# Sixteen state products of a Mamba layer: four of them moved from VectorE to GpSimd, in a four-part network kernel

## The reference, cut to what matters

```python
xz = x @ in_proj_w.T; xi, z = split(xz)                 # 2 x 256 channels
xc = silu(causal_conv(xi, 4 taps) + conv_b)
xp = xc @ x_proj_w.T                                     # dt_raw, B (16), C (16)
dt = softplus(dt_raw @ dt_proj_w.T + dt_proj_b)
dA = exp(dt * A[n]);  dBx = dt * xc * B[n]               # for each of 16 states n
h_n[t] = dA_n[t] * h_n[t-1] + dBx_n[t]                   # scan over 512 tokens
y = sum over n of h_n * C[n]  + xc * D
out = (y * silu(z)) @ out_proj_w.T
```

## Time and profile before

| | us |
|---|---|
| median of 3 runs | 2473.28 (2472.91 to 2476.75) |
| profiled execution, its own time | 2472.19 |
| its span in the trace | 2470.5 |
| Mamba stage, first scan to last gate product | 550.0 to 1730.9 |
| one pipeline iteration (start of a gate product y2 to the next), 14 of them from 627.63 to 1669.96 | 71.55 to 76.5, mean 74.5 |

### The profile page before, as it was taken

How to read it: one execution, slowest core, us unless ns; L and a number is a source line. 1 busy time by engine, 2 the same in 40 slices (tenths; PEclk the granted TensorE clock), 3 DMA queues, 4 the chain that set the end, 5 groups by cost and what they waited for, 6 DMA issues and landing times. The chain is left out here.

```text
span 2470.5 us, 24903 instructions
## 1 busy us (share of the span) xinstructions
PE 1779.2 (72%) x6321; PEld 937.4 (38%) x6321; DVE 1824.4 (74%) x3163; ACT 947.6 (38%) x1562; POOL 920.8 (37%) x666
## 2 busy tenths in 40 slices
PE   4776103437877677777777777776699999999998
PEld 3454002313333223333323333232455555555555
DVE  4888792128888888788888888889466767666676
ACT  1322000124444555444545445553233433334343
POOL 1101205736576566566575665664000000000000
PEclk7999555569899999898999999999899999999999
DMA  6333102232202122112222011210000000000000
GB/s 171 100 110 97 31 1 35 38 94 77 69 22 82 73 81 81 44 46 77 77 81 81 21 69 77 73 73 5 13 13 14 9 13 13 8 17 8 13 13 9
DMA packets 94551, 125.52 MB, mean 51 GB/s; under 512 B 6576, under 2 KB 86096, under 8 KB 90064
## 3 DMA queue, kind: packets, MB, share of 16 engines
q1 hardware_dynamic: 79888, 115.88, 13.4%
q0 software_dynamic: 14592, 8.92, 2.8%
HBM read 98.81 MB, written 25.90 MB: 50 GB/s over the span
## 5 line engine op out<-in xcount | busy, mean ns | idle before, releaser
L574 POOL TENSOR_TENSOR dbx<-u,ball 128x1024 f32<-128x1024 f32 x256 | 603.7, 2379 | 165.0 <-DVE hst L1293 164.8
L1293 DVE TENSOR_TENSOR_SCAN hst<-bank,dbx 128x512 f32<-128x512 f32 x512 | 598.5, 1210 | 59.5 <-DVE prod L1309 33.5
L744 ACT ACTIVATE bank<-dt,aneg 128x511 f32<-128x511 f32 x512 | 352.3, 690 | 596.4 <-DVE hst L1293 595.0
L966 PE MATMUL bank<-prod,ident 128*128 128x512 f32 x1024 | 531.2, 645 | 16.8 <-DVE prod L1309 16.8
L1309 DVE TENSOR_TENSOR prod<-hst,bank 128x1024 f32<-128x1024 f32 x256 | 311.1, 1215 | 7.9 <-PE bank L966 2.9
L774 ACT ACTIVATE ha<-bank,w_b 128x512 f32<-128x512 f32 (+1 forms) x208 | 142.8, 687 | 409.0 <-PE bank L1034 409.0
L1333 DVE SCALAR_TENSOR_TENSOR hg<-bank,w_b,ha 128x512 f32<-128x512 f32 (+1 forms) x208 | 155.8, 749 | 181.0 <-PE bank L1036 128.2
L966 PEld LDWEIGHTS bank<-prod,ident 128*128 128x128 f32 x1024 | 209.7, 206 | 207.1 <-issue 162.9
L956 PE MATMUL bank<-parts,sel_c 128*128 128x512 bf16 x256 | 105.0, 411 | 252.6 <-DVE prod L1309 250.7
L1034 PE MATMUL bank<-x3T,w_w 128*128 128x512 f32 (+1 forms) x416 | 224.5, 622 | 0.0
L1036 PE MATMUL bank<-x3T,w_w 128*128 128x512 f32 (+1 forms) x416 | 215.3, 599 | 0.0
(11 more groups left out here) (205 smaller groups left out, 2272.6 us busy)
## 6 DMA issues: line engine op xcount, KB each, us to landing
ball<-b_rows SPq DMA_DIRECT2D x32, 2048.0 KB, 9.4
xg_rows<-xg SPq DMA_DIRECT2D x16, 320.0 KB, 2.5
xt<-in_x SPq DMA_DIRECT2D x16, 256.0 KB, 2.9
xT<-in_xT SPq DMA_DIRECT2D x16, 256.0 KB, 3.1
resid_rows<-zero SPq DMA_DIRECT2D x16, 256.0 KB, 3.2
resid_rows<-resid SPq DMA_DIRECT2D x16, 256.0 KB, 2.4
rin<-resid_rows SPq DMA_DIRECT2D x16, 256.0 KB, 11.5
rin<-resid_rows POOLq DMA_DIRECT2D x16, 256.0 KB, 4.7
```

Source lines behind the costliest of these rows:

```text
L574: gp.tensor_tensor(dbx[n % NDB][:, :, :], u[s.par][:, :, :], ball[s.par][:, n:n + 1, :].to_broadcast([P, NH, SEQ]), ALU.mult).then_inc(dbx ...
L744: act.activation(da_ps[h][:, 1:SEQ], dt_[s.par][:, h, 1:SEQ], ACT.Exp, scale=aneg[:, h, n:n + 1]).then_inc(da_rdy, 1)
L966: last = mm(y_ps[:, h, :], ident[:, :], prod[n % 2][:, h, :], start=False, stop=(n == NS - 1), skip_group_check=True)
L1293: dve.tensor_tensor_scan(hst[:, h, :], da_ps[h][:, :], dbx[n % NDB][:, h, :], 0.0, ALU.mult, ALU.add).then_inc(scan_rdy, 1)
```

## The change

States 1, 4, 7 and 10 (`ON_POOL`) get their product with C on GpSimd (`weigh_c`), in the step of their scan, from a third state buffer `hst[2]` into a third product buffer `prod[2]`. GpSimd reads its C rows from SBUF: the four come by DMA from the stored rows (now B and C, 32 rows) into `call`, once its four products of the sequence before are made. For the other twelve states VectorE takes two state buffers and two product buffers in turn, counted by `place(n)`. TensorE leaves out the four spreads and adds the products of GpSimd one step later than before. VectorE's front work moves one step later, and with it the second gate projection on TensorE (9 to 10), its tanh on ScalarE (10 to 11), the middle parts on ScalarE (9 to 10, ahead of the logarithm), and dt and u on GpSimd (11, 12 to 12, 13). `ball` is one tile instead of two; its second half is loaded once dbx of all 16 states of the sequence before are made. The diff:

```diff
...
 AHEAD = 2
+ON_POOL = (1, 4, 7, 10)
+NP = len(ON_POOL)
+ND = NS - NP
 Z_EPS = 1e-6
...
+
+def place(n):
+
+    return sum(a < n for a in ON_POOL) if n in ON_POOL else n - sum(a < n for a in ON_POOL)
...
         x3_d = nc.dram_tensor("x3_rows", (TOK, D), F32).ap()
-        b_d = [nc.dram_tensor(f"b_rows{p}", (NS, SEQ), F32).ap() for p in range(2)]
+        b_d = [nc.dram_tensor(f"b_rows{p}", (2 * NS, SEQ), F32).ap() for p in range(2)]
...
             parts = [mb(f"parts{p}", [P, SEQ], BF16) for p in range(2)]
-            ball = [mb(f"ball{p}", [P, NS, SEQ]) for p in range(2)]
+            ball = mb("ball", [P, NS, SEQ])
+            call = mb("call", [P, NP, SEQ])
             dtr = mb("dtr", [P, NH, SEQ])
...
             dbx = [mb(f"dbx{k}", [P, NH, SEQ]) for k in range(NDB)]
-            hst = mb("hst", [P, NH, SEQ])
-            prod = [mb(f"prod{k}", [P, NH, SEQ]) for k in range(2)]
+            hst = [mb(f"hst{k}", [P, NH, SEQ]) for k in range(3)]
+            prod = [mb(f"prod{k}", [P, NH, SEQ]) for k in range(3)]
             y2 = mb("y2", [P, NH, SEQ])
...
         st_b, cb_rdy, da_rdy, dbx_rdy, scan_rdy = sem("st_b"), sem("cb_rdy"), sem("da_rdy"), sem("dbx_rdy"), sem("scan_rdy")
-        ld_b = [[sem(f"ld_b{p}{q}") for q in range(2)] for p in range(2)]
-        prod_rdy, y_mm, y2_rdy, res_mm, op_mm = sem("prod_rdy"), sem("y_mm"), sem("y2_rdy"), sem("res_mm"), sem("op_mm")
+        ld_b = [sem(f"ld_b{q}") for q in range(2)]
+        prod_rdy, pprod_rdy, yp_mm, ld_c, y_mm, y2_rdy, res_mm, op_mm = sem("prod_rdy"), sem("pprod_rdy"), sem("yp_mm"), sem("ld_c"), sem("y_mm"), sem("y2_rdy"), sem("res_mm"), sem("op_mm")
         m_mv, m_rs, x3_rdy, st_x30, st_x31 = sem("m_mv"), sem("m_rs"), sem("x3_rdy"), sem("st_x30"), sem("st_x31")
...
                 settle(sp)
-                sp.dma_start(b_d[s.par][:, :], xbc[0:NS, :]).then_inc(st_b, 16)
+                sp.dma_start(b_d[s.par][:, :], xbc[:, :]).then_inc(st_b, 16)
                 sp.wait_ge(st_b, s.at(16, 16))
-                settle(sp)
-                need(sp, dbx_rdy, s.at(NS, -NS))
                 settle(sp)
...
                     n = q * NS // 2
-                    sp.dma_start(ball[s.par][:, n:n + NS // 2, :],
+                    need(sp, dbx_rdy, s.at(NS, n - NS // 2))
+                    settle(sp)
+                    sp.dma_start(ball[:, n:n + NS // 2, :],
                                  b_d[s.par][n:n + NS // 2, :].rearrange("(a n) t -> a n t", a=1).to_broadcast([P, NS // 2, SEQ])
-                                 ).then_inc(ld_b[s.par][q], 16)
+                                 ).then_inc(ld_b[q], 16)
+                need(sp, pprod_rdy, s.at(NP))
+                settle(sp)
+                sp.dma_start(call[:, :, :], b_d[s.par][NS + ON_POOL[0]:NS + ON_POOL[-1] + 1:ON_POOL[1] - ON_POOL[0], :]
+                             .rearrange("(a n) t -> a n t", a=1).to_broadcast([P, NP, SEQ])).then_inc(ld_c, 16)
...
                     gp.wait_ge(u_rdy, s.at(1, 1))
-                gp.wait_ge(ld_b[s.par][n * 2 // NS], s.half(16, 16))
+                gp.wait_ge(ld_b[n * 2 // NS], s.at(16, 16))
                 need(gp, scan_rdy, s.at(NS * NH, NH * (n - NDB + 1)))
                 gp.tensor_tensor(dbx[n % NDB][:, :, :], u[s.par][:, :, :],
-                                 ball[s.par][:, n:n + 1, :].to_broadcast([P, NH, SEQ]), ALU.mult).then_inc(dbx_rdy, 1)
+                                 ball[:, n:n + 1, :].to_broadcast([P, NH, SEQ]), ALU.mult).then_inc(dbx_rdy, 1)
+
+            def weigh_c(s, n):
+                k = place(n)
+                if k == 0:
+                    gp.wait_ge(ld_c, s.at(16, 16))
+                gp.wait_ge(scan_rdy, s.at(NS * NH, NH * (n + 1)))
+                need(gp, yp_mm, s.at(NP, k))
+                gp.tensor_tensor(prod[2][:, :, :], hst[2][:, :, :], call[:, k:k + 1, :].to_broadcast([P, NH, SEQ]), ALU.mult
+                                 ).then_inc(pprod_rdy, 1)
...
                         spread_u(f, n + AHEAD - NS)
-                    if f and n == 11:
+                    if s and n in ON_POOL:
+                        weigh_c(s, n)
+                    if f and n == 12:
                         gp.wait_ge(dtl_rdy, f.at(1, 1))
...
                         gp.tensor_tensor(dt_[f.par][:, :, :], dtr[:, :, :], dta[:, :, :], ALU.add).then_inc(dt_rdy, 1)
-                    if f and n == 12:
+                    if f and n == 13:
                         gp.wait_ge(dt_rdy, f.at(1, 1))
...
                     act.activation(tc[:, :], pb_ps[:, :], ACT.Tanh).then_inc(tc_rdy, 1)
-                if n in (6, 10):
-                    h = (n - 6) // 4
+                if n in (6, 11):
+                    h = (n - 6) // 5
                     act.wait_ge(z_mm, s.at(NH, h + 1))
...
                     act.activation(xbc[:, :], pc_ps[0:2 * NS, :], ACT.Copy).then_inc(xbc_rdy, 1)
-                    need(act, cb_rdy, s.at(NS, -NS))
+                    need(act, cb_rdy, s.at(ND, -ND))
                     act.activation(parts[s.par][:, :], pc_ps[:, :], ACT.Copy).then_inc(xhi_rdy, 1)
...
                     act.activation(dta[:, :, :], dta[:, :, :], ACT.Exp, scale=-1.0).then_inc(dte_rdy, 1)
+                if n == 10:
                     act.wait_ge(xr_rdy, s.at(1, 1))
...
                     last.then_inc(cv_mm, 1)
-                if n in (5, 9):
-                    h = (n - 5) // 4
+                if n in (5, 10):
+                    h = (n - 5) // 5
                     if h == 0:
...
             def spread_c(s, n):
-                if n == 0:
+                k = place(n)
+                if k == 0:
                     pe.wait_ge(parts_rdy, s.at(1, 1))
-                need(pe, prod_rdy, s.at(NS, n - 1))
-                mm(cb_ps[n % 2][:, :], sel_c[:, n, :], parts[s.par][:, :], start=True, stop=True).then_inc(cb_rdy, 1)
+                need(pe, prod_rdy, s.at(ND, k - 1))
+                mm(cb_ps[k % 2][:, :], sel_c[:, n, :], parts[s.par][:, :], start=True, stop=True).then_inc(cb_rdy, 1)
...
             def add_state(s, n):
-                pe.wait_ge(prod_rdy, s.at(NS, n + 1))
+                k = place(n)
+                if n in ON_POOL:
+                    pe.wait_ge(pprod_rdy, s.at(NP, k + 1))
+                    from_, done = prod[2], yp_mm
+                else:
+                    pe.wait_ge(prod_rdy, s.at(ND, k + 1))
+                    from_, done = prod[k % 2], y_mm
                 for h in range(NH):
-                    last = mm(y_ps[:, h, :], ident[:, :], prod[n % 2][:, h, :], start=False, stop=(n == NS - 1),
+                    last = mm(y_ps[:, h, :], ident[:, :], from_[:, h, :], start=False, stop=(n == NS - 1),
                               skip_group_check=True)
-                last.then_inc(y_mm, 1)
+                last.then_inc(done, 1)
...
                         add_state(m, NS - 1)
-                    if s and n < NS - 1:
+                    if s and n < NS - 1 and n + 1 not in ON_POOL:
                         spread_c(s, n + 1)
...
                         skip_term(s)
-                    if s and n:
+                    if s and n - 2 in ON_POOL:
+                        add_state(s, n - 2)
+                    if s and n and n - 1 not in ON_POOL:
                         add_state(s, n - 1)
...
             def front(s, n):
-                if n in (3, 5):
-                    h = (n - 3) // 2
+                if n in (4, 6):
+                    h = (n - 4) // 2
                     dve.wait_ge(tc_rdy, s.at(NH, h + 1))
                     stt(xc[s.par][:, h, :], tc[:, :], 1.0, pb_ps[:, :], ALU.add, ALU.mult).then_inc(xc_rdy, 1)
-                if n == 10:
+                if n == 11:
                     dve.wait_ge(xmid_rdy, s.at(1, 1))
                     tt(parts[s.par][96:P, :], xr[96:P, :], parts[s.par][96:P, :], ALU.subtract).then_inc(parts_rdy, 1)
-                if n in (6, 11):
-                    h = (n - 6) // 5
+                if n in (7, 12):
+                    h = (n - 7) // 5
                     dve.wait_ge(tz_rdy, s.at(NH, h + 1))
...
                     stt(zs[s.par][:, h, :], tz[:, :], 1.0, pc_ps[:, :], ALU.add, ALU.mult).then_inc(zs_rdy, 1)
-                if n == 8:
+                if n == 9:
                     dve.wait_ge(xhi_rdy, s.at(1, 1))
...
             def gated(s):
-                dve.wait_ge(y_mm, s.at(NS, NS))
+                dve.wait_ge(y_mm, s.at(ND, ND))
+                dve.wait_ge(yp_mm, s.at(NP, NP))
                 need(dve, op_mm, s.at(1))
...
                 for n in range(NS):
+                    k = place(n)
+                    h_of = hst[2 if n in ON_POOL else k % 2]
                     if s:
                         dve.wait_ge(dbx_rdy, s.at(NS, n + 1))
-                        need(dve, prod_rdy, s.at(NS, n))
+                        if n in ON_POOL:
+                            need(dve, pprod_rdy, s.at(NP, k))
+                        else:
```

(11 more changed lines are left out.)

## The result

The changed kernel takes 2442.3 us (median of 4 runs, 2442.0 to 2444.3) against 2473.1: a ratio of 0.9874, 95% interval 0.9857 to 0.9892. It is faster by 31 us, 1.3%, clear of the scatter of the runs; forecast were 145, with 2385 as the upper end of the range.

A forecast was written before the change was run, and what follows sets the result against it. VectorE's own list, 85% busy in the loop, was taken as the bound. Twelve loop iterations at 10.5 us (126), plus 19, 9 and 5, made 159; less 14 of slack, 145 off 2472.2 gave 2327, forecast 2328, range 2303 to 2385.

The forecast's parts named there:

- the paragraph on the port: VectorE's parts beside GpSimd's product 10: delay between 0 and 2.35 us, taken as 0; scans and products lose nothing.
- wait for decay 12: ScalarE's decay, behind the logarithm, ends at 1195.3 with VectorE ready at 1194.1: a new wait of 1.3 us.
- the slack: 1 us in each of 14 iterations, 14 us, for handoffs (dbx 4, xc, decay 10) that won't all hold.
- TensorE's chain: TensorE's convolutions, states 1 to 3 and a spread, from 1159.48, end at 1173.6, leaving xc slack of 0.4 us.
- 7.1 with half of 4.5: The 1 MB load of `call`, behind the second half of `ball`, lands by 9.7 us, at 1212, before its use.
- rival B: GpSimd paces the stage: operations take 2.84 us, an iteration some 69, total 2397; chance 0.06.
- Front a step later: VectorE's four front waits for tanh and copies (xc, zs, xr) go: 6.0 us an iteration.
- State buffers: With two state buffers, VectorE's turn from product to next scan falls from 0.19 to 0.03 us.
- Products on GpSimd: Three products leave VectorE between the statistics and scan 12: 4.3 us less an iteration, against the new wait of 1.3.
- GpSimd as the bound, a late `call`: GpSimd fits with 56.2 of 63.2 us; a load some 20 us late would eat the gain, 2473, chance 0.03.
- Rival A: TensorE paces the front, partly at slow clock, or parts gets blocked: 2 to 4 us return, 2355 to 2385; chance 0.22.
- Rival C: GpSimd and VectorE exclude one another wherever both run: 3.57 us per GpSimd operation, 10 us more an iteration, 2612; chance 0.03.

The follow-up runs named there:

- experiments 5: Changed kernel, DMA issue left at step 6, plus one GpSimd wait for its own dbx 12 ahead of product 10: 2310.7 us, 0.9340.
- experiment 3: Changed kernel with GpSimd's DMA issue at step 1, ahead of idle time, instead of step 6: 2312.7 us, 0.9343.
- experiment 2: Kernel before, with VectorE making parts at step 12 instead of 10: 2486.4 us, ratio 1.0044.
- experiment 4: Kernel before with parts at step 12 and GpSimd's DMA issue moved from step 6 to the end of step 11: 2609.5 us, 1.0546.

## Why the prediction was wrong

*The failed step* is in the paragraph on the port: for the delay of parts it set the bounds "0 and 2.35; I take 0", that is one GpSimd operation at most. It had the right instruction and the right resource. But both the bound and the working by the rule of the Trainium skill (SBUF — State Buffer, Who interferes with whom) took the block to end with the operation that holds the port. It lasted for the rest of an overlapping run: 12.8 us in 13 of 16 iterations, 3.6 and 1.3 with an earlier pause, 9.2 in the kernel before with the issue moved. Against 0.69 that is 12.1 us an iteration; the 1.3 us wait for decay 12 is covered by it and gone. In all that is 13 x (12.1 - 1.3) = 140 us. Without the block the measured time is 2310.7 to 2312.7 (experiments 5 and 3), 130 us under 2442, so that 10 us of the account stay open.

*The rest of the sum* came out by some luck. With the block taken out, the kernel is 15 to 17 us under the forecast of 2328, and its mean iteration is 64.5, where 63.2 and 1 of slack were forecast. But the terms differ from the forecast both ways, as the next three paragraphs show, and the slack, set down for handoffs such as dbx 4 and xc, stands in other waits: 1.79 us ahead of y2 in the iteration shown, 35.5 us in all at the statistics in experiment 3. Two small sums are off as well and change nothing: TensorE's chain ends at 1173.5 by its own terms, not 1173.6, and 7.1 with half of 4.5 is 9.4, not 9.7.

*Read and not used:* the 2.84 us of the dbx beside the DMA issue stood there, and was priced as slowness, in rival B. It was overlap: starts stayed 2.30 apart. GpSimd was never slow.

*Front a step later*: 6.0 us an iteration forecast, 5.6 measured, or 88.6 us in all where 14 x 6.0 = 84 were expected. Right, and so was the order of what TensorE and ScalarE deliver.

*State buffers*: forecast at 0.16 a turn, 1.6 an iteration for the ten turns that the changed kernel has left, which would be 2.4 for the fifteen of an iteration with all products on VectorE. Measured there: 3.0. Under-sized: the turn went from 0.19 to -0.09, 0.28 instead of 0.16, some 4.2 in fifteen; part of that is lost again at the projection, where the statistics wait 20.3 us in 13 places, against 7.0 in five before.

*Products on GpSimd*: 4.3 less the new wait of 1.3, 3.0; measured 1.3, or 1.9 if the 27 us are shared out over 14 iterations. A product that follows its scan directly starts 0.19 behind it in the kernels with products on GpSimd, 0.03 in the one without (10.4 us in 54 places in experiment 3; why stays open). TensorE's projection eats product 1, as forecast: the statistics wait 35.5 us in 14 iterations, 2.5 each. Two other waits in experiment 3 are 21.0 us for decay 12, 1.5 each where 1.3 was forecast, and 15.7 for dbx, which the forecast left to the slack.

*GpSimd as the bound, a late `call`*: in the changed kernel VectorE waits 1.3 us in all for dbx, and product 1 waits for its scan, not for the load, apart from 8.1 us of `issue` in two places. With the block gone GpSimd is closer to a bound: the 15.7 us for dbx, 3.5 at the longest.

*Rival A* gave 2355 to 2385 with a blocked `parts` worth 2 to 4 us; its clause "or parts gets blocked" is what happened, at three to six times the size (12.1 us). *Rival C*, the exclusion of the two engines, was ruled out for scans and products, rightly (they stayed at 2.33 and 1.22 beside a busy GpSimd), but the rival didn't ask about the one instruction that it holds for.

## What to carry to other kernels

Before work moves to GpSimd, list the VectorE instructions with two SBUF inputs that will meet a busy GpSimd, and look at GpSimd's recorded lengths there against the distance of its starts. In this kernel, where they were longer by 0.45 us, such an instruction didn't get in until the run ended, and has to be priced at the rest of the run; where they were longer by 0.05, it got in at the next boundary. A wait of GpSimd for its own last operation (0.23 us) or a DMA issue placed ahead of idle time brought the lengths back, and was worth 130 us here. Making `parts` on GpSimd itself was not measured. A block of this kind counts as busy time, so read mean durations against those of before, not the waits alone.

## What the runs showed of the hardware

- A VectorE instruction with two SBUF inputs, against GpSimd operations that read SBUF: 0.69 us alone, 0.79 to 1.62 (medians) where GpSimd's operations are 2.35 long and start 2.30 apart, 9.2 and 12.8 where they are 2.75 to 2.83 long and start 2.30 apart; it ends 0.56 after the run does, whether it has lasted 1.4, 3.6, 9.2 or 12.8 us.
- A DMA issued by GpSimd leaves its next operations overlapping, as recorded, by some 0.45 us instead of 0.05 for as long as they follow without a pause: from 1165.60 to 1191.41 in the changed kernel, through eleven operations. The Trainium skill (GPSIMD Engine Reference, When to use GPSIMD) says that two of the engine's cores write the descriptors of such a DMA; that the cores then run out of step would fit, and no run here shows the cores one by one.
- GpSimd isn't slowed while `parts` is shut out; where `parts` gets in, it is GpSimd that pays: u starts on time and the next operation 0.47 late (experiment 2).
- The Trainium skill (SBUF — State Buffer, Who interferes with whom) calls the port pair that VectorE and GpSimd share an exclusive lock, and says of VectorE's 2-port modes that whoever issues first has it for the whole instruction and the other fully blocks. The traces agree for operations in step, where `parts` gets in at the next boundary, and differ where GpSimd's overlap: there three later GpSimd operations (experiment 4) or five (the changed kernel) go ahead of a `parts` that had been waiting since before them.
